# Flamingo layer with mixture of experts: attention of batches 14 and 15 written as one hand-ordered program

## What is computed

```python
x = x + tanh(g_xattn) * xattn(layernorm(x), ctx)       # 16 heads of 16 channels, softmax over 256 context tokens
h = layernorm(x)
bids = sigmoid(h @ conf_w.T + conf_b) * wealth         # 8 experts
top_bids, chosen = top_k(bids, 2); w = softmax(top_bids)
x = x + tanh(g_ffn) * sum_e combine[e] * ((silu(h @ gate_w[e].T) * (h @ up_w[e].T)) @ down_w[e].T)
```

## Time and profile before

| | us |
|---|---|
| three runs, median | 1085.46 |
| lowest, highest | 1083.96, 1087.34 |
| the profiled execution | 1083.07 |
| its span | 1081.4 |

### The profile page before, as it was taken

The page is one execution under the profiler, slowest core; times in us unless marked ns, Lnnn a source line. Parts: engine busy times, 40 slices in busy tenths (PEclk is TensorE's granted clock), DMA queues, the critical chain, the costliest instruction groups (busy, mean ns, idle before and its releaser), DMA issues.

```text
span 1081.4 us, 25127 instructions
## 1 busy us (share of the span) xinstructions
PE 1001.3 (93%) x8750; PEld 855.2 (79%) x8750; DVE 610.8 (56%) x1519; ACT 502.0 (46%) x796; POOL 366.3 (34%) x439
## 2 busy tenths in 40 slices
PE   5789999999999997759999999999999999999993
PEld 4556777777777765448999999999799999999993
DVE  3556777777777776455544444444554444444452
ACT  4366777777777774334323232332433323233321
POOL 1124555555555552443322212121332212122121
PEclk8799999999999999869999999999999999999997
DMA  8000111111111119258712111121262212121211
GB/s 254 27 22 22 43 45 47 41 41 41 43 51 58 41 39 371 77 182 323 256 25 40 25 35 35 25 37 23 42 229 49 37 23 40 20 40 23 37 35 17
DMA packets 48338, 77.30 MB, mean 71 GB/s; under 512 B 8616, under 2 KB 42152, under 8 KB 44456
## 3 DMA queue, kind: packets, MB, share of 16 engines
q0 software_dynamic: 18080, 50.15, 16.7%
q1 hardware_dynamic: 30216, 26.62, 8.3%
HBM read 52.09 MB, written 24.40 MB: 71 GB/s over the span
## 4 chain that ended last, share of the span: by engine, by line
PE 81%; ACT 5%; issue 4%; DVE 3%; POOL 3%; DMA 1%; SPq 1%; POOLq 1%; ACTq 0%; DVEq 0%
PE gate L1485 17%; PE up L1485 17%; PE down L1499 11%; PE down L1501 6%; PE pv L590 4%; PE scores L579 4%; PE misc L486 4%; PE scores L540 3%; PE maxps L554 2%; PE misc L513 2%; PE misc L522 2%; POOL K_rest L1204 2%; ACT probs L771 1%; PE misc L624 1%; PE turned L1468 1%
## 5 line engine op out<-in xcount | busy, mean ns | idle before, releaser
L1937 POOL DMA_INDIRECT out<-y,token x64 | 100.9, 1577 | 424.8 <-DVE y L1806 323.8
L1696 ACT ACTIVATE silu<-gate 128x512 f32<-128x512 f32 x128 | 76.8, 600 | 281.6 <-PE up L1485 281.6
L984 DVE TENSOR_REDUCE max_neg<-maxps 128x4 f32<-128x1024 f32 x128 | 156.5, 1222 | 60.2 <-PE maxps L554 60.2
L1485 PE MATMUL gate<-x_hi,w_split 128*128 128x256 f32 x1024 | 185.0, 282 | 2.0 <-DVE x_lo L1772 1.6
L1797 DVE TENSOR_TENSOR h<-silu,up 128x512 f32<-128x512 f32 x128 | 88.1, 688 | 174.8 <-ACT silu L1696 174.8
L1499 PE MATMUL down<-w_split,h_hi 128*128 128x512 f32 x512 | 185.9, 398 | 0.0
L1485 PE MATMUL up<-x_hi,w_split 128*128 128x256 f32 x1024 | 184.4, 282 | 0.0
L771 ACT ACTIVATE probs<-scores 128x1024 f32<-128x1024 f32 x124 | 127.2, 1026 | 80.5 <-PE scores L579 79.5
L1485 PEld LDWEIGHTS gate<-x_hi,w_split 128*128 128x128 f32 x1024 | 149.4, 189 | 5.5 <-issue 2.7
L1485 PEld LDWEIGHTS up<-x_hi,w_split 128*128 128x128 f32 x1024 | 148.8, 189 | 0.0
L1501 PE MATMUL down<-w_split,h_lo 128*128 128x256 f32 x512 | 144.1, 281 | 0.0
(11 more groups left out here) (204 smaller groups left out, 1586.3 us busy)
## 6 DMA issues: line engine op xcount, KB each, us to landing
stage<-gate_up_T POOLq DMA_DIRECT2D x20, 1024.0 KB, 8.1
stage<-down_T POOLq DMA_DIRECT2D x10, 1024.0 KB, 11.1
xg<-dispatched SPq DMA_DIRECT2D x34, 272.0 KB
ctxT<-ctxT SPq DMA_DIRECT2D x17, 256.0 KB, 2.8
x_all<-x SPq DMA_DIRECT2D x16, 256.0 KB, 5.2
out<-x_all SPq DMA_DIRECT2D x16, 256.0 KB, 2.2
dispatched<-pads SPq DMA_DIRECT2D x4, 272.0 KB, 3.6
dispatched<-pads POOLq DMA_DIRECT2D x4, 272.0 KB, 4.3
```

Of the source, the lines that this page charges most:

```text
L984: V.tensor_reduce(to, maxps[:], AX.X, ALU.max, negate=True).then_inc(s["max_taken"], 1)
L1485: last = mm(bank[:, i, :], into_inner(w, pair, mat)[:, c, cols], r[:, c, :], start=m == 0, stop=m == len(terms) - 1)
L1696: nc.scalar.activation(silu[pair % 2][:], gate[pair % 2][:], ACT.Silu).then_inc(s_silu, 1)
L1937: pool.indirect_dma_start(out, bass.IndirectOffsetOnAxis(token[:, t:t + 1], axis=0), y[:, t, :], None, compute_op=ALU.add).then_inc(s_adde ...
```

## The change

Batches 14 and 15 leave `body` and get a `last_two` on each engine. `Use` gets a prefix `of`, so that one list of `misc` banks, `LAST_TWO`, serves both batches (`END` for the back work of 13, `NEXT_BACK` for that of 14).

- TensorE: in batch 14, pair by pair, scores of 14 and maxima of 15; of batch 13's back work only `turn_heads` and `turn_normed` stay between them, `attn_out` comes behind `turn_maxima`. `turn_x2(13)`, `logits(13)`, `ranks(12)` go to batch 15, together with all of batch 14's back work up to `logits(14)`, and `ranks(13)`.
- VectorE: the maxima follow each other; `first_choice(12)` stays ahead, `second_choice(12)`, `residual(13)`, `positions(12)` and the rest come after `read_maxima`.
- ACT: the same order of batches' work as on TensorE.
- GpSimd: `load_ahead` stands before `scatter(12)`, not behind it.
- SyncE: `store_shift(15)` stands before the store of batch 13's residual; the store of 14's waits for the landing of 14 stores as before.

The diff, cut:

```diff
+        LAST_TWO = ["V", "TO0", "TO1", "TN", "MT", "WO", "next TO0", "next TO1", "RK", "next TN", "next WO", "TX2", "LG", "KNOWN",
+                    "next TX2", "next RK", "next LG"]
+        END = Use(LAST_TWO, after_all(full_use(BATCHES - 3)))
+        NEXT_BACK = Use(LAST_TWO, after_all(full_use(BATCHES - 3)), of="next ")
...
-            body(BATCHES - 2, 0, ITER14, False, True, True, True)
-            body(BATCHES - 1, 1, ITER15, False, False, True, True)
+            last_two()
...
+            def last_two():                      # SyncE
+                store_shift(Z, Z % 2, END)
+                store_residual(B, END)
+                sp.wait_ge(s["x2_stored"], 16 * C)
+                store_residual(C, NEXT_BACK)
...
+                project_v_in_parts(Z, 1, END)    # TensorE
+                scores_and_maxima(0)
+                turn_heads(B, 0, END)
+                turn_heads(B, 1, END)
+                scores_and_maxima(1)
+                scores_and_maxima(2)
+                weigh(C, 0, 0)
+                scores_and_maxima(3)
+                turn_normed(END)
+                scores_and_maxima(4)
...
+                exps(Z, 6)                       # ACT
+                norm_x2(C, 0)
+                exps(Z, 7)
+                read_pv(Z, 2)
+                second_weight(B)
...
+                for pair in range(2, HPAIRS):    # VectorE
+                    maxima(Z, pair)
+                read_maxima(Z, END)
+                second_choice(A)
+                residual(B, END)
+                norm_heads(C, 0, NEXT_BACK)
+                norm_heads(C, 1, NEXT_BACK)
+                positions(A, 0, END)
+                residual(C, NEXT_BACK)
+                read_logits(B, END)
+                space_experts(END)
+                first_choice(B)
+                second_choice(B)
+                positions(B, 1, NEXT_BACK)
...
+                scale_x2(B)                      # GpSimd, behind the loads of experts 0 and 1
+                pool.wait_ge(s["shifted"], Z * (16 * HPP) + 16 * HPP)
+                pool.wait_ge(s["x2_stored"], 16 * C)
+                load_ahead(pool)
+                scatter(A, 0)
+                scale_x2(C)
+                scatter(B, 1)
```

More of the change, by code:

```diff
@@ L277, in written @@
             def written(self, eng, what):
-                eng.wait_ge(s["misc_written"], self.before + (self.order.index(what) + 1))
+                eng.wait_ge(s["misc_written"], self.before + (self.order.index(self.of + what) + 1))
             def read(self, eng, what):
@@ L689, in body @@
                 max_of_next(0)
-                if is_last(b):
-                    known_counts(use)
                 if back:
@@ L713, in body @@
                     turn_x(b + 2, use)
-                if is_last(b):
-                    use.read(pe, "KNOWN")
                 if late:
@@ L753, in count_rows, with last_two, scores_and_maxima @@
                 mm(EPILOGUE2.bank("COUNT")[:, 0, 0:EXPERTS], ones[:], macc[:], start=True, stop=True).then_inc(s["misc_written"], 1)
+            def last_two():
+                def scores_and_maxima(pair):
+                    score(C, 0, pair)
+                    max_scores(Z, 1, pair, units_before(C))
+                project_v_in_parts(Z, 1, END)
[8 more added lines that the diff above has]
+                scores_and_maxima(4)
+                weigh(C, 0, 1)
+                scores_and_maxima(5)
+                scores_and_maxima(6)
+                weigh(C, 0, 2)
+                scores_and_maxima(7)
+                turn_maxima(Z, END)
+                attn_out(END)
+                weigh(C, 0, 3)
+                score(Z, 1, 0)
+                turn_heads(C, 0, NEXT_BACK)
+                turn_heads(C, 1, NEXT_BACK)
+                score(Z, 1, 1)
+                ranks(A, END)
+                score(Z, 1, 2)
+                turn_normed(NEXT_BACK)
+                score(Z, 1, 3)
+                weigh(Z, 1, 0)
+                attn_out(NEXT_BACK)
+                score(Z, 1, 4)
+                turn_x2(B, 1, END)
+                score(Z, 1, 5)
+                weigh(Z, 1, 1)
+                logits(END)
+                known_counts(END)
+                score(Z, 1, 6)
+                turn_x2(C, 0, NEXT_BACK)
+                score(Z, 1, 7)
+                weigh(Z, 1, 2)
+                END.read(pe, "KNOWN")
+                ranks(B, NEXT_BACK)
+                weigh(Z, 1, 3)
+                logits(NEXT_BACK)
             pe.wait_ge(s["w_split"], 2)
-            over_batches(pe, body)
+            over_batches(pe, body, last_two)
             return (turn_last_heads, lambda: turn_normed(EPILOGUE), project_last_out,
@@ L1227, in body @@
             def body(b, par, use, ahead, nxt, back, late):
[L1228 to L1237, removed]
                 if ahead:
@@ L1259, in scatter_last, with scale_x2, last_two @@
                 pad_experts(pool, range(EXPERTS // 2, EXPERTS))
-            over_batches(pool, body)
+            def scale_x2(b):
+                scale_of(b, "scale2_chain", "ln2_stats", mv2, rstd2, shift2, "ln2_scaled")
+            def last_two():
+                pool.wait_ge(s["shifted"], C * (16 * HPP) + 16 * HPP)
+                for e in range(HELD):
+                    for n in range(3):
+                        load_third(pool, e, n, stage[e])
+                scale_x2(B)
[5 more added lines that the diff above has]
+                scatter(B, 1)
+            over_batches(pool, body, last_two)
             return (lambda: scale_of(BATCHES - 1, "scale2_chain", "ln2_stats", mv2, rstd2, shift2, "ln2_scaled"),
```

62 lines of the change are left out of this document (48 added, 14 removed).

## The result

The changed kernel takes 1091.97 us (median of 6 runs, 1088.63 to 1093.81); the kernel before, beside it, 1085.38 (6 runs, 1083.96 to 1087.46). The ratio is **1.0055, 95% interval 1.0035 to 1.0075**, which is 6.0 us slower; the medians lie 6.6 apart, the two profiled executions 7.6. The profiled execution took 1090.72 us, with a span of 1089.0 where it was 1081.4, and a mean granted clock of 0.963 (0.969).

What follows compares the result with a forecast made beforehand. The stretch was taken as bound by waits, not TensorE's throughput, with GpSimd's copy of `rows` deciding. +2.0 (later heads) and +2.3 (half clock) gave +4.3 on 1085.46: 1089.8 us, range 1084.0 to 1092.5, the forecast's own 1088.3 to 1092.5.

Steps and rivals of the forecast that it cites:

- Part 1: Batch 14: VectorE's maxima start 1.81 us apart, last end 414.5, 4.5 us earlier; transfer issued at 415.4.
- Part 2: Maxima's transfer amid loads of experts 0 and 1: 1.5 us added to 3.16, batch 15's scores at 420.1.
- Part 3: GpSimd's queue and scatter 12's landing behind the loads set batch 14's normalised row: 434.0, before 435.96.
- Part 4: End of batch 15: TensorE waits 5.5 us for the copy of `rows` behind scatter 13; last normalised heads +2.0 us.
- Part 5: Behind the wait for `rows`, to the last projection's end: half clock costs 2.3 us, including 0.3 further on.
- A: Maxima's transfer and residual's store land early, batch 14's row at 431.5: about 0, 1085.5 us; chance 0.18.
- B: Clock stays up behind the wait for the copy of `rows`: +2.0 us alone, 1087.5; chance 0.17.
- C: Copy of `rows` over before TensorE has turned batch 15's last heads, win kept: −3.7 us, 1081.8; chance 0.07.
- D: Store of batch 13's residual takes its full 9.8 us, row 4.6 later: about +9, 1094.5 us; chance 0.08.

Runs made afterwards that it cites:

- e7: Kernel before with the loads of experts 0 and 1 moved from batch 14's start to batches 0 and 1; ratio 1.0074.
- e8: Changed kernel with the copy of `rows` ahead of scatter 13 and the loads of experts 0 and 1 moved to batches 0 and 1; ratio 1.0076.
- e3: Changed kernel with expert 1's loads moved from batch 14's start to behind scale_x2(14), with expert 2's, scatter 12 ahead of them; ratio 1.0026.
- e5_fill7: Changed kernel with seven unneeded matmuls in TensorE's wait for the maxima, ahead of batch 15's scores; ratio 1.007.
- e11_copylate: Changed kernel with the copy of `rows` ahead of scatter 13 and expert 2's loads behind that copy, no filler matmuls; ratio 1.0004.
- e10_copyfilllate: Changed kernel with the copy of `rows` ahead of scatter 13, expert 2's loads behind that copy, seven filler matmuls in the wait for the maxima; ratio 0.9981.
- e6: Changed kernel with the copy of `rows` ahead of scatter 13 and seven filler matmuls in the wait for the maxima; ratio 1.0017.
- e1_copy: Changed kernel with one move on GpSimd: the copy of `rows` ahead of scatter 13 instead of behind it; ratio 1.0002.
- e9_copyfillswap: Changed kernel with the copy of `rows` ahead of scatter 13, seven filler matmuls, and scatter 12 ahead of expert 2's loads; ratio 1.0001.
- e12_bothfilled: e10_copyfilllate with five more filler matmuls between batch 15's seventh scores and the turn of batch 14's row; ratio to the kernel before 1.0018.

## Why the prediction was right

The time (1089.8 forecast, 1091.97 measured), the sign and the place are right: TensorE waits for the copy of `rows`, and that makes the kernel slower. The size owes something to luck. Up to the turn of the last normalised heads the loss is 6.9 us where the sum had 2.0, a term behind it was too large by 1.6, and the two profiled executions lie 7.6 us apart, outside of the +2.8 to +7 that I gave; the medians' 6.6 and the ratio's 6.0 lie inside.

- **Part 1, the maxima close up: right.** 1.83 apart for 1.81, last end 414.24 for 414.5, transfer issued at 415.16 for 415.4.
- **Part 2, the transfer in traffic: right direction, too small.** Issue to scores took 5.83 us; 4.66 were assumed (3.16 + 1.5). Scores at 420.99, not 420.1. A quiet transfer takes 2.65 (e7, e8; 2.66 in e3). The hardware queue, which carries SyncE's transfers, shows no packet at all from 415 to 419, while the software queue is at 95 to 106% of the 16 engines; then 11 up to 419.75, and 57 in the next quarter of a microsecond, as the loads end. Most of those 57 must be the residual's store, which SyncE issued at 417.25: the two transfers show as 32 packets in e3_half (417 to 419).
- **Part 3, the row of batch 14: the step that failed.** Forecast 434.0, measured 437.49. The queue was estimated well (loads 421.82 for 422.7, scatter 12 at 428.22 for 427.0), but it was not what came last. The row needs `residual(14)` too, and so TensorE's projection; the sum had no such path. I counted half clock for the heads only, and it lasted through everything up to the projection: 1.97, 1.93 and 2.94 us for heads, `weigh` and projection instead of 1.09, 1.07 and 1.99. By e5_fill7, which has the scores at the same moment, this costs 4.6 us until the projection's end, and with the landing out of the way it costs the row 3.3 us (e11_copylate against e10_copyfilllate), nearly all of the 3.5 by which the row missed the forecast. GpSimd's and the landing's limit, which the prediction had put first, stands right behind: it is what e5, e6 and e8 ran into.
- **Part 4, the copy: mechanism right, size 4.9 short.** The wait was forecast as 5.5 us and is 5.59. It starts and ends 5 us later, since the row was late by 3.5 and the stretch from the row to the heads took 7.15 us (437.49 to 444.64), not 5.6: behind the 2.10 us gap the clock was halved once more, which I had counted as gone. The end of the wait hangs on `ranks(13)` in that same stretch, at 442.05 where the sum had 437.1. So the turn of the last normalised heads came 6.9 us later than before (452.18 for 445.27), where the sum had +2.0.
- **Part 5, the clock behind that wait: mechanism right, size too large.** From 6.9 it goes to 7.6 by the end of the span; the term was 2.3. Up to the end of the last projection the clock did cost what the part says, in kind: that stretch takes 5.04 us (452.18 to 457.22) where it took 3.58 (445.27 to 448.85, at a granted clock of 1.00), so 1.5 more, where the term had 2.0 for it (and 2.9 for half clock throughout). Behind it, where the term had 0.3 more, 0.8 comes back, since the kernel before loses more there than the changed one, which I hadn't counted. From the turn of batch 15's row it runs at 0.55 (454.34 to 462.00), the changed kernel at 0.70 (462.61 to 470.30). TensorE before, then after:

```profile
454.34 1.12 PE L474 MATMUL misc<-idn,row 128*128 128x128 f32 x4 [2.31 <-ACT row L794]
```
```profile
455.04 2.18 PE L620 MATMUL misc<-wo_s,oT 128*128 128x256 f32 x8
...
462.61 0.66 PE L482 MATMUL misc<-idn,row 128*128 128x128 f32 x4 [2.21 <-ACT row L846]
```

- **The rivals.** A (early landing) fell: it had 3.2 us from issue to scores, and 5.83 were measured. With it falls the use that the prediction made of the Trainium skill (DMA: Bandwidth & Descriptors, "Queues, rings and completion order"), that turns taken between the queues leave a small transfer nearly undisturbed: for the 4 us from 415 to 419 the hardware queue shows no packet. B (clock stays up) fell at 421.46. C (the gain is kept) fell, and e1_copy and e10 show what it lacked: the copy ahead of scatter 13. Even then, of the 4.8 us by which the maxima are earlier, e10 keeps 2.1. D (9.8 us for the store) fell: 4.0.
- Still open: by the ratio the copy explains all 6.0 us, by positions after the landmark 3.0 to 4.9 of 7.9. The kernel before has only one profile here, and the part behind row 15 takes 625.1 to 628.7 us from kernel to kernel, so I don't divide it further.

## What to carry to other kernels

An early step that gets faster pays only if the step that is last on another engine's queue moves too: look for what is queued in program order ahead of a small copy that the next stage needs, and move the copy first (here worth 0.5%). Bulk loads issued from the same queue as small writes on whose landing an engine waits belong behind those writes, and not beside a load that is wanted at once either: e9_copyfillswap, with them straight behind the scatter, had to wait for `xg`. And when one limit is removed, say which is next before building on it: here they were copy, landing of scatter 12, load of `xg`, landing of scatter 13.

## What was not expected of the hardware

- A gap of 3.58 us in TensorE's work is followed by 11.5 us without any idleness at a clock of 0.56 (0.50 from 425 to 430, 0.69 from 430 to 432.50); in e5_fill7 9.40 us at 0.50 behind 5.67 us of idleness. With 0.46 us of idleness in its place the same instructions run at full clock. Gaps of 2.10 to 2.66 us ahead of batch 14's row are followed by half clock too: the turn takes 1.11 to 1.12 for 0.66, and in e3_half, where it still takes 0.66 behind 2.62 us, the `weigh` after it takes 1.93. Behind 0.61 us the clock stays full.
- How long it stays down isn't told by the gap. In e1_copy and in the changed kernel TensorE has the same instructions behind the same 2.10 us; in e1_copy all 8.39 us up to the heads run at 0.50, in the changed kernel the clock is at 0.89 over 441.00 to 444.60 and the heads are at full clock. Why is open, and it is 1.9 us at the heads, as much as several of the effects studied here.
- Two DMAs of 8 KB under a software queue full of packets of 8 KB (98.4% of the 16 engines' time over 412 to 420) took 5.83 us from issue to use, 2.65 in quiet; scatters behind the 3 MB on their own queue have landed by 13.4 to 14.7 us after the loads' issue (423.00 to 436.45 in e5_fill7, 442.21 to 456.86 in e12_bothfilled, to the start of the row that waits for them).
- The same code takes up to 3.7 us more or less over the first two batches from one profiled execution to the next (68.93 to 72.64), as much as most effects studied here.
